# A four-layer attention and expert network on one core: the last attention in pairs of batches, and the last layer with its gate products first and one GpSimd step per piece

## The chip, the cores and the metric

The kernel runs on one core of one Trainium2 chip. A core has TensorE (PE: matrix products and turns), VectorE (DVE), ScalarE (ACT), GpSimd (POOL) and SyncE (SP, which here only issues DMAs). Each engine runs its own list of instructions in order and waits on semaphores. The time is the device time of one execution in microseconds; a lower one is better.

## The reference

Input are 16 batches of 128 tokens with 128 features, all float32, and a context `ctx_1024` of the same shape. There are four layers, each `x = x + attention(norm(x))` and then `x = x + feed-forward(norm(x))`. Three of the feed-forwards are mixtures of experts and hold most of the work. The change touches only the last attention and the last feed-forward:

```python
    x = x + _L3_xattn_ref(_layernorm(x, axis=-1), ctx_1024, ctx_1024, pos_1xS2)
    x = x + _L3_ffn_ref(_layernorm(x, axis=-1), L3_ffn_w_gate, L3_ffn_w_up, L3_ffn_w_down)
```

The attention has one head of 128. Two score matrices are made per batch, one with a positional table added to queries and keys (`pe[pos]`), one with other rows of that table (`pe[s_g_pos]`, `pe[g_pos]`); a fixed mask says per pair of positions which of the two counts, and the rest is causal:

```python
        attn = jnp.where(mask.astype(bool), ngb_attn, g_attn)
        w = jax.nn.softmax(attn, axis=-1)
        return jnp.einsum('bqk,bkd->bqd', w, v)
```

The feed-forward is a gated one, 128 to 384 and back, in which activations are rounded to 16 bits with a scale taken over the whole tensor:

```python
        def act_qdq(x):
            qmax = 2.0 ** (ACT_BITS - 1) - 1.0
            scale = jnp.maximum(jnp.max(jnp.abs(x)) / qmax, 1e-12)
            return jnp.clip(jnp.round(x / scale), -qmax - 1.0, qmax) * scale
        ...
        x = act_qdq(x)
        up = act_qdq(x @ lpbq_dequant(w_up).T)
        gate = act_qdq(x @ lpbq_dequant(w_gate).T)
        sig = fixed_qdq_u16(jax.nn.sigmoid(gate))
        gate = act_qdq(gate * sig)
        o = act_qdq(gate * up)
        return o @ lpbq_dequant(w_down).T
```

So five times a largest value over everything must be known before the next step can start: of x, up, gate, gate * sig, and o.

## The kernel before

Five engine programs are written out by hand, one per engine, and joined by semaphores. Stages have names: `l0x, l0f, l0m, l1x, l1f, l1m, l2x, l2m` are the attentions, inner attentions and expert layers of the first three layers; `l3x` is the last attention and `l3m` the last feed-forward. The tokens live in `X`, `[128 tokens, 16 batches, 128 features]`. There are eight PSUM banks of 512 columns: four `score_bank`, `turn_bank`, `out_bank` and two `f_bank`.

*End of l2m.* VectorE adds the experts' outputs to `X` in four chunks (`add`, L1927), takes the statistics of each batch (`measure`, L1597) and the variances (`variances`, L1606 and on); GpSimd takes the root (`power`, L702).

*l3x* runs batch by batch. The order of the steps on every engine is the table `ORDER["l3x"]`, in which Y is the normalising, F the queries and keys, S the scores, E the exponential, T the turn and V the weighing. Per batch: SyncE loads `cT` (L653) and `V128` (L657), 64 KB each. VectorE normalises the tokens into `y_tok` (L1689), TensorE turns them (L1188), VectorE adds the two positional tables (L1769, L1770), GpSimd adds two to the keys (L773, L774). TensorE puts the masks into a bank by a bf16 product (L1341) and adds two score products beside each other (L1343). VectorE copies one half (L1707), takes the maximum with the other (L1709: the mask has made the one that doesn't count very low), the largest value of a row (L1712), and subtracts it (L1716). ScalarE takes the exponential (L976), TensorE turns it (L1349), ScalarE copies it (L982), TensorE weighs the values (L1357) with a column of ones beside them, whose result is the sum. VectorE takes its reciprocal (L1723) and adds the scaled result to `X` (L1725), waits on it (L1732) and takes the new statistics.

*l3m* has these steps, each ended by a largest value (VectorE, L2029), an all-reduce over partitions (GpSimd, L911) and a few small steps on VectorE (`scale`):
- VectorE normalises 16 batches (L1633), one largest value over 2048 columns; TensorE turns the tokens (L1370), ScalarE rounds by adding a large number (`MAGIC`, 1.5 x 2^23; L1116), VectorE takes it off (L2037).
- 24 products of 512 columns (L1571) by two banks, three of up and three of gate for each of four chunks of tokens; ScalarE copies each out (L1122), VectorE takes the largest value of each. Both all-reduces follow together.
- Six pieces of 1024 columns (`HIDDEN_ORDER`): ScalarE rounds gate (L1127), up (L1127), and takes the sigmoid (L1134); VectorE takes MAGIC off gate (L2055), rounds the sigmoid (L2064), multiplies (L2066) and takes the largest value. GpSimd takes MAGIC off up (L920) and multiplies by up's scale (L921), two steps with two inputs each.
- ScalarE rounds again, VectorE multiplies with up (L2076), largest value.
- Rounding by VectorE and ScalarE in halves (L2087, L2088), the last product (L1579: 48 of 128x128, two records each), VectorE adds to `X` (L2092), SyncE stores (L669).

Where GpSimd goes from elementwise steps to an all-reduce or back, its instruction list has a row `ISA` without operands: the switch.

## Time and profile before

| | us |
|---|---|
| median of 3 runs (1544.35 to 1546.91) | 1546.83 |
| the profiled execution | 1546.87 |
| its span | 1545.1 |
| TensorE busy in the span | 1302.3 (84%) |
| VectorE | 987.3 (64%) |
| ScalarE | 726.6 (47%) |
| GpSimd | 499.0 (32%) |

The span goes from the first instruction to the last; the profiled execution's own time holds also what lies around it. The granted clock is the share of TensorE's full speed that the chip allowed; the mean here is 0.915, but the last stages stand apart. A row of a timeline is one instruction or a run of like ones: start, duration, engine, line, output and inputs, and in brackets how long its engine stood idle before it and what ended that. Matrix products of float32 leave more than one record each. In rows grouped by line the last field is the idle time before them.

### The profile page before, as it was taken

Reading aid. Unit: us, or ns where it says so; the run is one execution under the profiler, and the core shown is the slowest. Engines: PE = TensorE matmul, PEld = TensorE weight load, DVE = VectorE, ACT = ScalarE, POOL = GpSimd, SP = SyncE. Lnnn points to the kernel's source line nnn. Section 1 sums busy time; section 2 is a strip of 40 time slices with the busy share of each in tenths; the row PEclk is TensorE's granted clock in tenths of the full one; section 3 lists DMA queues with packets and bytes.
Section 4 is the critical chain, followed back from the end, with each engine's and each line's share of the span. In section 5 each row is a group of like instructions: output and inputs, shape, how many; then the busy total and the mean of one; then the engine's idle time right before and its main releaser. Section 6 shows DMA issues by size and latency. Waiting matters only on the chain.

```text
span 1545.1 us, 29908 instructions
## 1 busy us (share of the span) xinstructions
PE 1302.3 (84%) x9616; PEld 932.9 (60%) x9616; DVE 987.3 (64%) x2308; ACT 726.6 (47%) x2096; POOL 499.0 (32%) x544
## 2 busy tenths in 40 slices
PE   4888789999979999979988999889969799966603
PEld 3676677777755666557776777656645566644203
DVE  2766366676766555666775666656677845568696
ACT  3666156565634444447775777522212233321542
POOL 6500266666625000052213222120040057732070
PEclk9999699999999999999999999979988799965856
DMA  7000000000005555510000000012210066501000
GB/s 260 8 8 19 1 1 1 0 0 0 1 1 165 187 190 191 186 48 2 0 0 2 1 0 0 2 47 85 85 58 1 1 169 165 146 23 32 0 0 27
DMA packets 40086, 81.68 MB, mean 53 GB/s; under 512 B 5411, under 2 KB 22851, under 8 KB 39893
## 3 DMA queue, kind: packets, MB, share of 16 engines
q1 hardware_dynamic: 40020, 80.84, 16.7%
q8 instruction: 37, 0.61, 0.2%
q14 instruction: 29, 0.23, 0.1%
HBM read 79.18 MB, written 1.64 MB: 52 GB/s over the span
## 4 chain that ended last, share of the span: by engine, by line
PE 61%; DVE 14%; ACT 14%; issue 7%; POOL 2%; DMA 1%; ACTq 0%; DVEq 0%; SPq 0%; POOLq 0%
PE score_bank L1414 15%; ACT h_all L939 10%; PE f_bank L1443 7%; PE f_bank L1178 5%; PE score_bank L1259 5%; PE turn_bank L1275 4%; PE out_bank L1443 3%; PE turn_bank L1443 3%; PE out_bank L1315 3%; PE out_bank L1284 2%; PE score_bank L1250 2%; PE f_bank L1571 1%; PE out_bank L1324 1%; DVE work L1658 1%; PE f_bank L1199 1%
## 5 line engine op out<-in xcount | busy, mean ns | idle before, releaser
L1414 PE MATMUL score_bank<-parts 128*128 128x512 f32 x1040 | 396.2, 504 | 8.6 <-DVE parts L1792 7.1
L939 ACT ACTIVATE h_all<-score_bank,top_score 128x128 f32<-128x128 f32 x896 | 281.6, 401 | 114.7 <-DVE top_score L1646 114.6
L1414 PEld LDWEIGHTS score_bank<-parts 128*128 128x128 f32 x1040 | 202.2, 195 | 161.0 <-issue 115.0
L1646 DVE TENSOR_REDUCE top_score<-score_bank 128x4 f32<-128x512 f32 x224 | 142.9, 680 | 136.8 <-PE score_bank L1259 136.8
L1443 PE MATMUL f_bank<-h_all,wset 128*128 128x512 f32 x260 | 136.6, 607 | 14.7 <-DVE h_all L1889 12.9
L1877 DVE TENSOR_TENSOR h_all<-work,h_all 128x512 f32<-128x512 f32 x124 | 91.2, 738 | 85.8 <-ACT h_all L1043 85.7
L1043 ACT ACTIVATE h_all<-score_bank,wset 128x512 f32<-128x512 f32 x128 | 87.8, 687 | 116.1 <-PE score_bank L1414 116.0
L1275 PE MATMUL turn_bank<-CF,h_all 128*128 128x128 f32 x512 | 83.4, 286 | 42.7 <-DVE work L1658 23.2
L702 POOL TENSOR_TENSOR small<-small,half_neg 128x4 f32<-128x4 f32 (+2 forms) x22 | 36.3, 1655 | 241.3 <-DVE small L1619 128.6
L1275 PEld LDWEIGHTS turn_bank<-CF,h_all 128*128 128x128 f32 x512 | 56.3, 144 | 69.1 <-ACT h_all L939 22.7
L1039 ACT ACTIVATE rope_c<-score_bank 128x512 f32<-128x512 f32 x66 | 39.4, 597 | 112.6 <-PE score_bank L1414 99.4
L939 ACT ACTIVATION_READ_ACCUMULATOR h_all<-score_bank,top_score 128x1 f32 x384 | 91.9, 239 | 0.0
L1259 PEld LDWEIGHTS score_bank<-work 32*128 32x128 f32 (+1 forms) x2304 | 77.8, 187 | 22.9 <-issue 21.8
L1259 PE MATMUL score_bank<-work 32*128 32x128 f32 (+1 forms) x2304 | 90.0, 281 | 1.5 <-issue 1.2
L722 POOL TENSOR_TENSOR h_all<-h_all,prob_rec 128x512 f32<-128x512 f32 x64 | 66.3, 1046 | 75.1 <-DVE prob_rec L1650 75.1
L1039 ACT ACTIVATE shifted<-score_bank 128x512 f32<-128x512 f32 x66 | 39.3, 597 | 93.4 <-PE score_bank L1414 83.4
L1889 DVE TENSOR_TENSOR h_all<-score_bank,shifted 128x512 f32<-128x512 f32 x66 | 45.5, 691 | 43.8 <-POOL shifted L900 35.7
L1178 PE MATMUL f_bank<-yT,big 128*128 128x128 f32 x512 | 68.8, 285 | 1.4 <-ACT yT L996 1.4
L1579 PE MATMUL f_bank<-W3T,big 128*128 128x128 f32 x96 | 12.5, 298 | 67.6 <-DVE big L2088 67.6
L1443 PE MATMUL out_bank<-h_all,wset 128*128 128x512 f32 x130 | 66.3, 593 | 2.0 <-DVE h_all L1877 1.1
L1443 PE MATMUL turn_bank<-h_all,wset 128*128 128x512 f32 x130 | 67.2, 598 | 0.0
L1889 DVE TENSOR_TENSOR h_all<-score_bank,rope_c 128x512 f32<-128x512 f32 x66 | 45.4, 688 | 32.9 <-POOL rope_c L900 16.3
(360 smaller groups left out, 2748.4 us busy)
## 6 DMA issues: line engine op xcount, KB each, us to landing
work<-gates_l0m SPq DMA_DIRECT2D x62, 512.0 KB, 3.7
W0X<-gates_l2m SPq DMA_DIRECT2D x32, 256.0 KB, 3.8
CTX<-gates_l2m SPq DMA_DIRECT2D x32, 256.0 KB, 3.8
wset<-in_l0m SPq DMA_DIRECT2D x32, 128.5 KB, 3.4
W0X<-gates_l1m SPq DMA_DIRECT2D x8, 512.0 KB, 3.6
wset<-in_l1m SPq DMA_DIRECT2D x8, 384.0 KB, 3.1
CTX<-gates_l1m SPq DMA_DIRECT2D x6, 512.0 KB, 3.7
cT<-in_ctxT SPq DMA_DIRECT2D x32, 64.0 KB, 1.8
```

The source lines that it names most:

```text
L722: pool.tensor_tensor(probs4, probs4, wide(prob_rec[c][:, :], HEADS, P), ALU.mult).then_inc(normed, 1)
L939: last = act.activation(held[c][:, P * m:P * m + P], score_bank[c][:, P * m:P * m + P], ACT.Exp, bias=top_score[c][:, m:m + 1], **sums)
L1039: act.activation(act_sb[at][:, :], hid_bank[(c * H + h) % 2][:, :], ACT.Silu).then_inc(acted, 1)
L1043: act.activation(hT[at][:, :], hid_bank[at][:, :], ACT.Gelu, bias=wslot(M, s)[:, 2 * P:2 * P + 1]).then_inc(acted, 1)
L1178: last = pe_.matmul(bk[:, cols + P * q:cols + P * q + P], w[:, P * (m + q):P * (m + q) + P], x[:, :], start=True, stop=True)
L1259: last = pe_.matmul(banks[c][:, P * m:P * m + P], qT[slot][rows * c:rows * c + rows, at:at + P], kT[slot][rows * c:rows * c + rows, kat:ka ...
L1275: last = pe_.transpose(turn_dest(L, u)[:, P * m:P * m + P], held[unit_slot(L, u, s)][:, P * m:P * m + P], ident)
L1414: last = pe_.matmul(bk[:, :], wt[s % 2][:, col:col + P], y[:, x], start=(part == 0), stop=(part == len(parts_of) - 1))
L1443: pe_.matmul(sum_bank[c][:, :], wslot(M, s)[:, at:at + P] if n != "l2m" else wset[s][:, at:at + P], hT[(c * H + h) % 4][:, :], start=first ...
L1646: dve.tensor_reduce(top_score[c][:, :], split(score_bank[c][:, :], HEADS), AX_X, ALU.max, negate=True)\
L1877: dve.tensor_tensor(tile_at[:, :], by, tile_at[:, :], ALU.mult).then_inc(gated if M["gated"] else h_made, 1)
L1889: dve.tensor_tensor(hT[at % 4][:, :], hid_bank[2 + at % 2][:, :], act_sb[at % 4][:, :], ALU.mult).then_inc(h_made, 1)
```

## The change

*Loads.* The context comes once, whole: `ctxT` twice, into the two halves of `keys3` (a part of `work`), and `ctx` into `AO`, 3 MB in all, issued by SyncE behind the first weight loads of l2m. VectorE adds the positional tables to the keys inside l2m's first two sets of experts (`place_keys`, eight steps of 512 columns).

*End of l2m.* All four `add(c)` now stand behind the last expert step, and the normalising of l3x goes by quarters of four batches. GpSimd adds two small steps to each root (L701, L702 of the new file), so that ScalarE can normalise by scale and bias (`normalise`).

*l3x* runs by pairs of batches: 4 score products and one mask product fill one bank (`score3`), VectorE takes both batches' largest values in one step of 512 columns (`largest3`), ScalarE takes the exponential of both halves with the sum (`exponentials3`), and TensorE joins the two halves by turning both into one place (`turn_probs3`), after two products that only fill (`stream`). There is no copy, maximum or subtraction on VectorE any more, nothing on GpSimd and no load.

*l3m*: ScalarE normalises, the largest value goes by quarters; 8 and 12 filler products stand ahead of the 24, 16 ahead of the last product. The 24 go gate first, over eight banks. The order of the all-reduces is tokens, gate, up, gate * sig, o. The rounding of gate and the sigmoids start after gate's scale; ScalarE rounds pieces 0 and 1 of up with the last gate pieces, 2 to 5 behind the last sigmoid. GpSimd only takes MAGIC off, one step with one input per piece (L905); up's scale goes into the scale of the product. The last rounding goes by quarters, 3 x 512 columns each.

The diff, cut to what the prediction speaks of:

```diff
@@ GpSimd
+                    if name in ("l3x", "l3m"):
+                        link(last)
+                        link(pool.tensor_tensor(less_mean[:, lo:hi], mean[:, lo:hi], r1[:, lo:hi], ALU.mult))
+                        last = pool.tensor_scalar(shift[:, lo:hi], less_mean[:, lo:hi], -1.0, None, ALU.mult)
...
-            for n, count in enumerate([1, 2, 1, 1]):
+            for n, at in enumerate((0, 2, 1, 3, 4)):
                 pool.wait_ge(step("l3m.part_max"), n + 1)
...
-                if n == 1:
-                    pool.wait_ge(step("l3m.scale"), 3)
+                pool.partition_all_reduce(quant[:, at, 1:2], quant[:, at, 0:1], P, bass.bass_isa.ReduceOp.max)\
+                    .then_inc(step("l3m.all_max"), 1)
+                if n == 2:
                     for at, h in enumerate(HIDDEN_ORDER):
                         pool.wait_ge(step("l3m.u_round"), at + 1)
-                        u = U3[:, :, :].rearrange("p m t -> p (m t)")[:, 1024 * h:1024 * h + 1024]
-                        link(pool.tensor_tensor(u, u, magic.to_broadcast([P, 1024]), ALU.subtract))
-                        pool.tensor_tensor(u, u, quant[:, 1, 2:3].to_broadcast([P, 1024]), ALU.mult).then_inc(step("l3m.u"), 1)
+                        part = work[:, 1024 * h:1024 * h + 1024]
+                        pool.tensor_scalar(part, part, -MAGIC, None, ALU.add).then_inc(step("l3m.u"), 1)
@@ ScalarE
+            for c in range(4):
+                copies(1, c)
+            copies(0, 0)
+            act.wait_ge(step("l3m.scale"), 2)
+            for at in range(6):
+                rounded(big, at, 2, "l3m.g_round")
+                if at < 3:
+                    copies(0, at + 1)
+                if at == 4:
+                    act.wait_ge(step("l3m.scale"), 3)
+                if at >= 4:
+                    rounded(U, at - 4, 1, "l3m.u_round")
+                sigmoid(at)
+            for at in range(2, 6):
+                rounded(U, at, 1, "l3m.u_round")
@@ TensorE
+            def score3(j):
...
+                pe_.matmul(bk[:, :], ident_bf, own_bf.unsqueeze(1).to_broadcast([P, 2, 2 * P]), start=True, stop=False, skip_group_check=True)
+                for x in range(2):
+                    b = 2 * j + x
+                    for m in range(2):
...
+                        last = pe_.matmul(bk[:, cols], queries3[j // 2 % 2][:, b % 4, m, :], keys3[:, b, m, :],
+                                          start=False, stop=True, skip_group_check=True)
...
+            for j in range(2, PAIRS):
+                score3(j)
+                weigh3(j - 2)
+                turn_probs3(j - 1)
+                if j in (2, 4):
+                    fronts3(j // 2 + 1)
@@ VectorE
+                def place_keys(t):
+                    dve.wait_ge(in_keys, 16 * 3)
...
+                    dve.tensor_tensor(two, two, places, ALU.add).then_inc(placed3, 1)
...
+            for j in range(2, PAIRS):
+                largest3(j)
+                if j in (3, 5):
+                    queries3_of(j // 2 + 1)
+                add3(j - 2)
```

How the rows stand on an engine. GpSimd, from the last roots to the end, before (L911 the all-reduce, L920 and L921 the two steps per piece of up):

```order
L702 TENSOR_TENSOR small<-small,half_neg 128x12
L702 TENSOR_TENSOR small<-small,half_neg 128x4
L911 ISA
L911 ISA quant<-quant 128x1 x3
L920 ISA
L920 TENSOR_TENSOR work<-work,CF 128x1024
L921 TENSOR_TENSOR work<-work,quant 128x1024
```

The pairs of L920 and L921 repeat to the sixth, then come `L911 ISA` and two more all-reduces. After (L898 the all-reduce, L905 the one step per piece):

```order
L697 TENSOR_TENSOR small<-small,half_neg 128x12
L701 TENSOR_TENSOR small<-small 128x12
L702 TENSOR_SCALAR small<-small 128x12
L697 TENSOR_TENSOR small<-small,half_neg 128x4
L701 TENSOR_TENSOR small<-small 128x4
L702 TENSOR_SCALAR small<-small 128x4
L898 ISA
L898 ISA quant<-quant 128x1 x3
L905 ISA
L905 TENSOR_SCALAR work<-work 128x1024 x6
L898 ISA
L898 ISA quant<-quant 128x1 x2
```

The number of switches is the same, three. The two roots of l3m, of 12 and of 4 batches, have each got two small steps behind them; the second switch and the third stand around six steps in place of twelve.

TensorE inside the attention, before: two batches (L1341 masks, L1343 scores, L1349 turn, L1188 tokens, L1357 weighing):

```order
L1341 MATMUL score_bank<-CB 128x256
L1343 MATMUL score_bank<-work 128x128 x2
L1349 MATMUL score_bank<-CF,h_all 128x128
L1188 MATMUL f_bank<-CF,y_tok 128x128
L1357 MATMUL out_bank<-V_1,h_all 128x129
```

After: one pair (L1562 masks, L1567 scores, L1591 weighing, L1352 filler, L1582 turn):

```order
L1562 MATMUL score_bank<-CB 128x512
L1567 MATMUL score_bank<-work 128x128 x4
L1591 MATMUL score_bank<-AO,h_all 128x128 x2
L1352 MATMUL turn_bank<-CB 128x512 x2
L1582 MATMUL turn_bank<-CF,h_all 128x128 x4
```

One round now serves two batches: the scores of a pair stand ahead of the weighing of the pair two before it and the turn of the one before it.

ScalarE in the rounding stage, before (L1127 rounding: `big` is gate, `work` is up; L1134 sigmoid into `CTX`):

```order
L1127 ACTIVATE big<-big,CF,quant 128x1024
L1134 ACTIVATE CTX<-big,quant 128x1024
L1127 ACTIVATE work<-work,CF,quant 128x1024
L1127 ACTIVATE big<-big,CF,quant 128x1024
L1134 ACTIVATE CTX<-big,quant 128x1024
L1127 ACTIVATE work<-work,CF,quant 128x1024
L1127 ACTIVATE big<-big,CF,quant 128x1024
L1134 ACTIVATE CTX<-big,quant 128x1024
L1127 ACTIVATE work<-work,CF,quant 128x1024
L1134 ACTIVATE CTX<-big,quant 128x1024
L1127 ACTIVATE big<-big,CF,quant 128x1024 x9
```

After (L1138 rounding, L1144 sigmoid):

```order
L1138 ACTIVATE big<-big,CF,quant 128x1024
L1138 ACTIVATE work<-work,CF,quant 128x1024
L1144 ACTIVATE CTX<-big,quant 128x1024
L1138 ACTIVATE big<-big,CF,quant 128x1024
L1138 ACTIVATE work<-work,CF,quant 128x1024
L1144 ACTIVATE CTX<-big,quant 128x1024
L1138 ACTIVATE work<-work,CF,quant 128x1024 x4
L1138 ACTIVATE big<-big,CF,quant 128x1024 x6
```

The roundings of up were one behind each gate piece; now two stand among the last gate pieces and four behind the last sigmoid, and GpSimd's step needs each.

## Rows read from the trace of the kernel before

**Rows 1.** windows; us, busy (x count) of PE, PEld, DVE, ACT, POOL, clock, DMA:

```profile
40.00:60.00 20.00, 16.88 (x145) 13.07 (x144) 15.53 (x25) 12.71 (x47) 19.56 (x8) 0.98 0.03 9
1210.00:1220.00 10.00, 10.00 (x48) 9.63 (x47) 8.30 (x24) 3.84 (x6) 0.07 (x1) 0.50 0.00 0
1369.00:1428.00 59.00, 40.81 (x143) 27.79 (x143) 45.41 (x190) 9.38 (x32) 16.75 (x34) 0.50 0.12 35
1435.80:1464.40 28.60, 24.77 (x56) 9.33 (x56) 19.29 (x35) 17.33 (x28) 0.67 (x2) 0.92 0.00 1
1464.40:1508.10 43.70, 0.00 (x0) 0.00 (x0) 37.95 (x30) 21.75 (x19) 29.26 (x13) 0.50 0.00 0
1508.10:1525.40 17.30, 0.00 (x0) 0.00 (x0) 15.13 (x18) 6.90 (x6) 0.35 (x1) 0.50 0.00 0
1525.40:1545.10 19.70, 12.52 (x96) 12.33 (x96) 9.09 (x13) 3.50 (x3) 0.00 (x0) 0.82 0.18 53
```

**Rows 2.** chain of waits, the attention; start us, us, what:

```profile
1390.76 0.87 PE score_bank L1343 x4
1397.58 0.87 PE score_bank L1343 x4
```

**Rows 3.** lines by form, attention, TensorE; busy us, mean ns, idle before:

```profile
L1343 PE MATMUL score_bank<-work 128*128 128x128 f32 x64 | 17.0, 421 | 0.0
...
L1357 PE MATMUL turn_bank<-V,h_all 128*128 128x129 f32 x16 | 6.4, 500 | 0.7 <-ACT h_all L982 0.7
...
L1341 PE MATMUL score_bank<-CB 128*128 128x256 bf16 x16 | 6.2, 389 | 13.0 <-DVE work L1770 11.2 <-POOL work L774 1.8
```

**Rows 4.** timeline, end of the rounding stage; start us, us, engine, what:

```profile
1498.53 2.38 DVE L2064 TENSOR_SCALAR CTX<-CTX 128x1024 f32<-128x1024 f32 x1
...
1503.34 0.68 DVE L2064 TENSOR_SCALAR CTX<-CTX 128x1024 f32<-128x1024 f32 x1
1504.06 1.23 DVE L2066 SCALAR_TENSOR_TENSOR big<-CTX,big 128x1024 f32<-128x1024 f32 x1
1505.32 1.22 DVE L2029 TENSOR_REDUCE part_max<-big 128x1 f32<-128x1024 f32 x1
```

**Rows 5.** windows, inside the last product:

```profile
1533.00:1536.00 3.00, 3.00 (x30) 3.00 (x29) 0.69 (x1) 0.00 (x0) 0.00 (x0) 1.00 0.24 67
```

**Rows 6.** timeline, TensorE before the last experts:

```profile
1199.94 0.60 PE L1370 MATMUL f_bank<-CF,Y 128*128 128x128 f32 x4
...
1203.55 1.89 PE L1364 MATMUL turn_bank<-CB 128*128 128x512 bf16 x8
```

**Rows 7.** part 5 of the page, a 512-wide maximum:

```profile
L1646 DVE TENSOR_REDUCE top_score<-score_bank 128x4 f32<-128x512 f32 x224 | 142.9, 680 | 136.8 <-PE score_bank L1259 136.8
```

**Rows 8.** lines by form, attention, VectorE:

```profile
L1725 DVE SCALAR_TENSOR_TENSOR X<-turn_bank,recips,X 128x128 f32 x7 | 2.4, 350 | 1.0 <-DVE recips L1723 0.2
```

**Rows 9.** timeline, between the last experts and the attention:

```profile
1359.54 0.87 DVE L1597 BATCH_NORM_STATS2 st<-X 128x6 f32<-128x128 f32 x4
...
1367.93 1.09 POOL L702 TENSOR_TENSOR small<-small,half_neg 128x4 f32<-128x4 f32 x1 [0.24 <-DVE small L1621]
```

**Rows 10.** timeline, GpSimd around its all-reduces:

```profile
1435.04 0.38 POOL L911 PARTITION_ALL_REDUCE quant<-quant  x1 [5.84 <-DVE quant L2029]
...
1471.01 1.92 POOL L920 TENSOR_TENSOR work<-work,CF 128x1024 f32<-128x1024 f32 x1 [6.94 <-issue]
...
1506.87 0.38 POOL L911 PARTITION_ALL_REDUCE quant<-quant  x1 [6.51 <-DVE quant L2029]
```

**Rows 11.** lines by form, GpSimd, whole span:

```profile
L836 POOL TENSOR_SCALAR big<-big,GCOL 128x1024 f32<-128x1024 f32 x3 | 8.7, 2884 | 0.3
...
L860 POOL TENSOR_SCALAR MASK<-MASK 128x2048 bf16<-128x2048 bf16 x1 | 1.9, 1900 | 0.1
```

**Rows 12.** timeline, VectorE in the first experts of l2m:

```profile
1242.17 0.69 DVE L1889 TENSOR_TENSOR h_all<-score_bank,rope_c 128x512 f32<-128x512 f32 x1 [6.28 <-PE score_bank L1414]
```

**Rows 13.** DMA issues; times issued, KB each, us to landing:

```profile
W0X<-in_w0x SPq DMA_DIRECT2D x1, 1024.0 KB, 7.1
```

More of the change, by code:

```diff
@@ new lines, in _, with copies, piece, rounded @@
+            U = work
+            def copies(w, c):
+                for m in range(3):
+                    e = 12 * (1 - w) + 3 * c + m
+                    act.wait_ge(products_made, e + 1)
+                    act.activation((U3, G3)[w][:, m, BANK * c:BANK * c + BANK], ring8[e % 8][:, :], ACT.Copy)\
+                        .then_inc(products_copied, 1)
+            def piece(t, at):
+                h = HIDDEN_ORDER[at]
+                return t[:, 1024 * h:1024 * h + 1024]
+            def rounded(t, at, n, signal):
+                act.activation(piece(t, at), piece(t, at), ACT.Identity, scale=quant[:, n, 3:4], bias=magic).then_inc(step(signal), 1)
@@ new lines, in _ @@
+            add(0)
+            measured(0)
+            add(1)
+            measured(1)
+            queries3_of(0)
+            add(2)
+            largest3(0)
+            measured(2)
+            largest3(1)
+            add(3)
+            queries3_of(1)
+            measured(3)
+            for j in range(2, PAIRS):
+                largest3(j)
+                if j in (3, 5):
+                    queries3_of(j // 2 + 1)
+                add3(j - 2)
+            variances("l3m", 0)
+            add3(PAIRS - 2)
@@ new lines, in _, with largest, join_max @@
+            add3(PAIRS - 1)
+            variances("l3m", 1)
+            def largest(dst, src):
+                return dve.tensor_reduce(dst, src, AX_X, ALU.max, apply_absolute_value=True)
+            def join_max(last, n, cols):
+                link(last)
+                largest(quant[:, n, 0:1], part_max[:, cols]).then_inc(step("l3m.part_max"), 1)
+            for g in range(4):
+                dve.wait_ge(step("l3m.y"), g + 1)
+                last = largest(part_max[:, g:g + 1], Y[:, 4 * g:4 * g + 4, :].rearrange("p b d -> p (b d)"))
@@ L2014, in scale @@
+            join_max(last, 0, slice(0, 4))
             def scale(n, waits, unit=None):
@@ L2067, in _ @@
                 dve.wait_ge(step("l3m.gs"), at + 1)
-                last = largest(part_max[:, at:at + 1], part)
-            product_max(last, 3)
+                return largest(part_max[:, at:at + 1], piece(big, at))
+            for c in range(4):
+                last = chunk_max(1, c)
+            join_max(last, 2, slice(12, 24))
+            chunk_max(0, 0)
+            scale(2, 2)
+            gate_steps(0)
+            chunk_max(0, 1)
+            gate_steps(1)
+            chunk_max(0, 2)
@@ new lines, in _, with quarter, round_quarter, scale_quarter @@
+                dve.wait_ge(step("l3m.p"), at + 1)
+                last = largest(part_max[:, at:at + 1], piece(big, at))
+            join_max(last, 4, slice(0, 6))
+            scale(4, 5, 5)
+            dve.wait_ge(step("l3m.scale"), 5)
+            def quarter(q):
+                return G3[:, :, BANK * q:BANK * q + BANK]
+            def round_quarter(q):
+                link(dve.tensor_scalar(quarter(q), quarter(q), quant[:, 4, 3:4], MAGIC, ALU.mult, ALU.add))
+            def scale_quarter(q):
+                dve.tensor_scalar(quarter(q), quarter(q), MAGIC, quant[:, 4, 2:3], ALU.subtract, ALU.mult).then_inc(hidden_ready, 1)
```

472 lines of the change are left out of this document (234 added, 238 removed).

## The prediction

> **What bounds the kernel now.** The forecast is made against the profiled execution: 1546.87 us, of which 1545.1 us are the span, so 1.8 us lie around it. The median of the runs shown, 1546.83 us, is the same number. The change acts behind 1358.8 us, so I read that stretch, first the busy time by stage [rows 1]. The reader sees six stages: the last attention (59.0 us from 1369.0), the normalising of tokens (7.8, the gap before the next row), 24 products with their copies (28.6), rounding and sigmoid (43.7), the largest product (17.3), the last product and the store (19.7). [...]
>
> The chain of waits then shows the attention's beat: the score products of one pair of batches stand 6.8 us after those of the pair before (1390.76, 1397.58) [rows 2]. By form and line, one pair holds on TensorE 4 score products at 0.42, and per batch a mask product 0.39 and a weighing 0.50 [rows 3], a turn and a transpose of the same 128x128 size as a score product: 4 x 0.42 + 2 x (0.39 + 0.50 + 0.84) = 5.1 us of 6.8. The other 1.7 us are hand-overs between engines, since every batch passes them one by one.
>
> In the rounding stage the timeline shows VectorE and GpSimd slowing each other: the same 1024-wide step takes VectorE 2.38 us where GpSimd works and 0.68 where it rests [rows 4]. GpSimd is not the end of that stage: its all-reduce waits for VectorE.
>
> **The attention.** Removed per batch: VectorE's copy, maximum and subtraction, GpSimd's two key additions, two small loads. A pair now needs on TensorE one 512-wide bf16 mask product, 4 score products, 2 weighings, 2 bf16 filler products (512 wide) and 4 turns with the halves joined; twice in six pairs 4 transposes. At the upper clock a 128x128 f32 product is about 0.22 us (30 records in 3.00 us at clock 1.00 [rows 5], two records a product, so 0.20, and a little for the gaps between groups), the filler 0.236 (eight in 1.89) and four transposes 0.60 [rows 6]. So: mask 0.23 + scores 0.89 + weighings 0.45 + fillers 0.47 + turns 0.89 = 2.93, with hand-overs 3.2 us. At the lower clock the same list is 0.46 + 1.68 + 1.0 + 0.94 + 1.68 = 5.8, with hand-overs and transposes 6.5.
> VectorE has per pair a 512-wide maximum 0.68 [rows 7], two scaled additions of 0.35 [rows 8], two statistics of 0.22 (four in 0.87 [rows 9]) and a reciprocal: about 2.1 us, 3.3 where the queries of a quarter come too. ScalarE has two exponentials and a copy, 1.7. So TensorE stays the bound, with work lined up in front of it.
> Which clock? The rows speak both ways: TensorE 10.00 of 10.0 us busy at 0.50, 16.88 of 20.0 at 0.98 [rows 1], and in the stage of the last product, whose mean is 0.82 [rows 1], 1.00 is reached by 1533, 4 us behind its start [rows 5]. The attention before was broken by waits at 0.69 busy and stayed low; the new one is nearly continuous with the fillers. I take the upper level. Other end: 6.5 instead of 3.2 for the six pairs, +20 us.
> The start is not free. Additions and statistics of l2m's four chunks now stand together behind its last step: first addition at about 1359.2, 0.69 and 0.87 for addition and statistics and 1.0 for the variances, a root 1.09 [rows 9] and 0.5 for the two new small GpSimd steps, four normalisings on ScalarE 1.1, transposes 1.2 (cold), queries 1.2: queries at 1366.7, then three cold score groups held by the additions to 1375.9. Six pairs of 3.2 with two transposes of 0.6, and the last turn and weighing, end at 1398.2; the additions at 1399.6, variances 1400.55, root 1402.05.
>
> **The library switch.** Behind the root GpSimd's first all-reduce came 5.84 us after VectorE's last word for it, and the first subtraction 6.94 us after GpSimd had nothing to wait for; but the all-reduce at 1506.87 follows VectorE's maximum at once (0.3 us), as its switch ran while GpSimd stood idle [rows 10]. So a change between elementwise work and all-reduce costs some 6 us wherever nothing hides it. The first stays: 1402.05 + 5.85 = 1407.9, against a maximum ready at 1404.2; scale ready 1408.7 (1435.84 before): 27.1 us earlier.
> [...]
>
> **Products.** 24 products took 22.8 us (24.77 less the 1.97 of turns) at clock 0.92 [rows 1]: 0.86 each warm. The gate's twelve go first, so its scale waits for 12, not 24: start 1410, end 1421, copies, maximum, all-reduce and scale to 1426.5. That is 17.8 us instead of 28.6, and the other twelve run under the next stage.
>
> **Rounding and sigmoid.** Costs with GpSimd at rest: ScalarE 1.15 per 1024 columns (six in 6.90 [rows 1]) and a hand-over, VectorE 0.68 each for taking the rounding number off the gate and for rounding its sigmoid, 1.23 for their product, 1.22 for its largest value [rows 4]. Counted from the gate's scale: ScalarE has nine copies of the late products among its first rounds, and the maxima over them keep VectorE until 15.1. Its first piece (0.68 + 1.23 + 1.22, 3.2 with gaps), the other scale 0.8 and one gate step 0.7 end at 19.8, pieces 1 and 2 with their gate steps (3.9 each) at 27.6. GpSimd's first two subtractions lie from 27.5 to 34.2 and hold VectorE, so that piece 3 ends near 36.2 instead of 30.8, and the last gate step at 36.9. Sigmoid 5 ends at 38.1; the other four roundings of u stand behind it on ScalarE, so GpSimd starts its third subtraction at 39.4.
> What is a one-input GpSimd step of 128x1024 f32? The row is 2.88 us (the mean of three) [rows 11]; the immediate form on bf16, 2048 wide, took 1.90, 0.93 ns an element [rows 11], so the other end is 0.95 us. I take 2.83, hardly under the row of the same type and size. Four of them end at 50.7; then the switch, 6.3, is exposed, as the third all-reduce is now queued behind the last subtraction: 57.0, scale 58.1. So 58.1 us instead of 43.7, +14.4: the halved GpSimd work costs more than it saves, because half of it waits for ScalarE and a switch stands behind it.
> [...]
>
> **The rest.** Largest product: 17.3 as before. Round and scale: quarters of 1536 on VectorE, 2.1 us to the first instead of 3.7, up to 3.4 if the strided form is slower. Last product at the upper clock after 16 fillers 10.7 (48 x 0.22) instead of 12.52 [rows 1]; if the fillers don't bring the clock up, 12.5 again; last addition and store 3.4 as before. 16.2 instead of 19.7.
> The 8 key additions of 0.69 us lie among the experts of l2m, where VectorE idles (6.28 us ahead of its step at 1242.17 [rows 12]): nothing, 5.5 us if that cover were gone. The loads of 3.1 MB stand before l2m's gates, where the queues carried nothing (1210 to 1220: 0 GB/s [rows 1]).
>
> **Sum.** Before, from 1358.8: 77.0 + 28.6 + 43.7 + 17.3 + 19.7 = 186.3. After: 49.9 + 17.8 + 58.1 + 17.3 + 16.2 = 159.3. That is 27.0 less; I add 2 us for hand-overs not seen: 1546.9 - 25 = 1522. Nearly all of it is the attention.
>
> **Rivals.**
> 1. TensorE stays at the lower clock through the attention. For: [rows 1], 10.00 busy at 0.50. Against: 0.84 busy at 0.98, and the climb in [rows 5]. +20: 1542.
> 2. GpSimd's immediate form runs at 0.93 ns an element. [...] Then the u pieces keep ScalarE's pace (1.15), VectorE is not blocked, and the stage is 11 us shorter: 1511. Against: the 2.88 of [rows 11].
> 3. Slower. The key loads land late and VectorE waits at its first key addition inside l2m's first sets, with every expert step queued behind it. It decides if they land after some 1261, which is 50 GB/s for 3.1 MB from 1198. At the attention's 35 GB/s [rows 1] they land at 1287, l2m starts some 50 us late: about 1570. Against: 1 MB landed in 7.1 us at the start [rows 13].
> 4. The clock low and the l3m switch both exposed beyond the sum (a second switch in front of the tokens' all-reduce waits for VectorE): +20 and 3 to 6: inside 1544 to 1550, no change.
>
> **Chances.** Forecast 0.62, with its own range 1513 to 1531; rival 2 0.12; rival 1 0.15; rival 4 0.06; rival 3 0.03, and 0.02 for other mishaps on the slower side. A measurement tells about 0.2% (3 us) from no change, so no change is 1543.7 to 1550. Of rival 1 a fifth (0.03) lies there, of rival 4 two thirds (0.04), its rest is slower: faster 0.62 + 0.12 + 0.12 = 0.86, same 0.07, slower 0.02 + 0.03 + 0.02 = 0.07. The range 1509 to 1543 reaches from beyond rival 2 to the middle of rival 1 and leaves out rivals 3 and 4 and the edges, about 2 in 10.
>
> **What would show it.** Right: the granted clock at 0.9 or more from about 1378 to 1398, pairs 3.2 us apart; scale of the tokens near 1409 with GpSimd idle 5.8 us before its first all-reduce; six GpSimd steps of 2.8 us and then 6 us idle before the third all-reduce, so a rounding stage near 58 us; the last product in 10.7 us. Wrong: clock 0.50 in the attention; GpSimd steps near 1 us; VectorE idle for DMA at its key additions near 1240; or a stage of l2m that is longer than before.

## The result

The changed kernel took 1506.70 us, median of 4 runs (1504.82 to 1515.58), against 1546.87 us before (1544.35 to 1551.95). The ratio is 0.9748, 95% interval 0.9701 to 0.9794: faster. Forecast were 1522 us and a range of 1509 to 1543, so the time lies below the range. The profiled execution took 1504.82 us, span 1503.0, mean granted clock 0.945.

The windows of the changed kernel by stage; columns as in [rows 1]. The eight are: additions behind l2m; the attention's start; its six pairs; the tokens' scale; the gate's twelve products; rounding and sigmoid; the largest product; last product and store.

```profile
1348.20:1356.30 8.10, 3.03 (x18) 1.78 (x16) 6.04 (x27) 4.07 (x10) 2.94 (x6) 0.91 0.00 0
1356.30:1369.50 13.20, 11.05 (x54) 10.02 (x56) 8.73 (x33) 7.43 (x21) 2.94 (x6) 0.67 0.00 1
1369.50:1389.30 19.80, 18.39 (x140) 16.51 (x142) 13.17 (x45) 8.34 (x31) 2.38 (x2) 1.00 0.01 1
1389.30:1399.90 10.60, 7.09 (x26) 4.00 (x27) 5.08 (x18) 6.26 (x16) 2.23 (x6) 0.68 0.01 2
1399.90:1417.80 17.90, 17.90 (x48) 8.10 (x47) 11.12 (x13) 11.74 (x19) 0.35 (x1) 1.00 0.00 0
1417.80:1468.20 50.40, 5.03 (x12) 1.90 (x10) 30.24 (x36) 26.12 (x28) 17.96 (x8) 0.59 0.00 0
1468.20:1485.90 17.70, 4.66 (x15) 1.93 (x16) 15.20 (x19) 6.91 (x6) 0.35 (x1) 0.54 0.00 0
1485.90:1503.00 17.10, 11.34 (x98) 10.79 (x96) 10.08 (x10) 3.23 (x2) 0.00 (x0) 0.96 0.22 62
```

Read against [rows 1]: the stretch from the first addition (1348.2) to the tokens' scale (1399.9) is 51.7 us where it was 77.0. The products up to the first scale that lets the rounding start are 17.9 (28.6), the rounding stage 50.4 (43.7), the largest product 17.7 (17.3), the end 17.1 (19.7). Together 154.8 us in place of 186.3: 31.5 us less. The other 10.6 us of the 42.1 by which the two spans differ lie ahead of 1348.2.

TensorE in the attention, changed kernel, by the timeline; each L1562 row opens a pair. The rows begin with the third of the eight pairs, the first of the six of the third window:

```profile
1365.03 0.61 PE L1562 MATMUL score_bank<-CB 128*128 128x512 bf16 x1 [2.02 <-DVE work L2057]
...
1369.98 0.38 PE L1562 MATMUL score_bank<-CB 128*128 128x512 bf16 x1
1370.19 1.05 PE L1567 MATMUL score_bank<-work 128*128 128x128 f32 x8
...
1373.16 0.39 PE L1562 MATMUL score_bank<-CB 128*128 128x512 bf16 x1
...
1376.49 0.38 PE L1562 MATMUL score_bank<-CB 128*128 128x512 bf16 x1
...
1379.67 0.39 PE L1562 MATMUL score_bank<-CB 128*128 128x512 bf16 x1
```

The first pair shown still takes 4.95 us (8 records of scores in 1.92 us, from 1365.42: the lower clock, 0.50 in the column from 1365.03 to 1367.00). Behind it the same 8 records take 1.05 at the upper clock (1.00 from 1372 to 1386), and pairs come 3.18, 3.33 and 3.18 us apart, where [rows 2] had 6.8.

GpSimd in the changed kernel, timeline:

```profile
1399.16 0.38 POOL L898 PARTITION_ALL_REDUCE quant<-quant  x1 [6.02 <-issue]
1415.25 0.35 POOL L898 PARTITION_ALL_REDUCE quant<-quant  x1 [15.71 <-DVE quant L2101]
1431.26 0.72 POOL L898 PARTITION_ALL_REDUCE quant<-quant  x1 [15.66 <-DVE quant L2101]
1442.40 2.82 POOL L905 TENSOR_SCALAR work<-work 128x1024 f32<-128x1024 f32 x1 [10.42 <-ACT work L1138]
1446.09 3.08 POOL L905 TENSOR_SCALAR work<-work 128x1024 f32<-128x1024 f32 x1 [0.88 <-ACT work L1138]
1450.07 10.97 POOL L905 TENSOR_SCALAR work<-work 128x1024 f32<-128x1024 f32 x4 [0.91 <-ACT work L1138]
1466.97 0.38 POOL L898 PARTITION_ALL_REDUCE quant<-quant  x1 [5.92 <-issue]
```

What [rows 10] showed is there in its new places: 6.02 us of idle ahead of the tokens' all-reduce and 5.92 ahead of the fourth (the third behind the tokens'), and in neither does the profile name an engine that it waited for. VectorE's maximum had been ready 2.2 us before the one (1396.98) and 12.6 us before the other. The steps of one input take 2.82, 3.08 and 10.97 / 4 = 2.74 us, as [rows 11] had it; most of the last four lie behind VectorE's last step. VectorE beside them:

```profile
1442.48 1.53 DVE L2149 TENSOR_SCALAR CTX<-CTX 128x1024 f32<-128x1024 f32 x1
...
1446.43 1.24 DVE L2143 TENSOR_SCALAR big<-big 128x1024 f32<-128x1024 f32 x1
...
1448.31 1.23 DVE L2150 SCALAR_TENSOR_TENSOR big<-CTX,big 128x1024 f32<-128x1024 f32 x1
...
1451.69 1.23 DVE L2150 SCALAR_TENSOR_TENSOR big<-CTX,big 128x1024 f32<-128x1024 f32 x1
...
1454.20 0.16 DVE L2101 TENSOR_REDUCE quant<-part_max 128x1 f32<-128x6 f32 x1
```

A product step (L2150) takes 1.23 us beside a working GpSimd (1451.69), and the sigmoid's rounding 1.53 in place of 0.69. Of VectorE's steps beside GpSimd only the three simple ones (TENSOR_SCALAR) that began near a GpSimd step's start are longer, by 0.84, 0.56 and 0.26 us (1.53, 1.24 and 0.95, the last at 1450.71); products and largest values keep their 1.23 and 1.22. VectorE was at its end at 1454.4 and waited 13 us for GpSimd.

### The profile page after: what moved, and what is told of

It is laid out like the page before. It is cut to its first block, busy times and chain, and to the rows that moved or that the text cites. A ratio compares the mean times of both kernels' runs of the same rounds, so it can differ in the third digit from the quotient of the medians.

```text
span 1503.0 us, 29518 instructions
## 1 busy us (share of the span) xinstructions
PE 1284.3 (85%) x9665; PEld 930.1 (62%) x9708; DVE 951.5 (63%) x2176; ACT 740.5 (49%) x2135; POOL 477.8 (32%) x518
## 3 DMA queue, kind: packets, MB, share of 16 engines
q1 hardware_dynamic: 36996, 81.89, 17.3%
## 4 chain that ended last, share of the span: by engine, by line
PE 61%; ACT 15%; DVE 12%; issue 7%; POOL 3%; DMA 1%; ACTq 0%; DVEq 0%; SPq 0%; POOLq 0%
PE score_bank L1402 15%; ACT h_all L922 10%; PE f_bank L1431 7%; PE f_bank L1195 5%; PE score_bank L1273 5%; PE turn_bank L1289 4%; PE turn_bank L1431 3%; PE out_bank L1431 3%; PE out_bank L1329 3%; PE out_bank L1298 2%; PE score_bank L1264 2%; PE out_bank L1338 1%; DVE work L1730 1%; PE f_bank L1216 1%; DVE top_score L1718 1%
## 5 line engine op out<-in xcount | busy, mean ns | idle before, releaser
L1195 PEld LDWEIGHTS f_bank<-yT,big 128*128 128x128 f32 x512 | 63.2, 198 | 4.7 <-issue 3.1
L1431 PEld LDWEIGHTS f_bank<-h_all,wset 128*128 128x128 f32 x260 | 49.4, 192 | 26.6 <-DVE h_all L1918 12.3
```

The costliest lines, as they stand in the source:

```text
L1195: last = pe_.matmul(bk[:, cols + P * q:cols + P * q + P], w[:, P * (m + q):P * (m + q) + P], x[:, :], start=True, stop=True)
L1431: pe_.matmul(sum_bank[c][:, :], wslot(M, s)[:, at:at + P] if n != "l2m" else wset[s][:, at:at + P], hT[(c * H + h) % 4][:, :], start=first ...
```

## The experiments

Theory 1: the rounding stage came out shorter than forecast because a GpSimd step of one input hardly holds VectorE. Theory 2: most of the time gained ahead of the last experts is not the change's; it is when TensorE's clock rises in an execution. The rivals stand in the expectations. All ratios are to the kernel before.

**The changed kernel again**, unchanged.

> The changed kernel once more, unchanged. In its first profile the gates of l2m were ready at 1223.95 us, 9.7 us earlier than before the change (1233.66), in a part of the program whose work is the same. Theory A: those 9.7 us are when TensorE's clock was granted in that one execution; then this profile shows another time there, between 1224 and 1234, and the ratio to before comes out nearer to the 0.983 of the stages behind it than 0.975. Rival B: the change causes it; then the gates come at 1224 within 1.5 us, and the ratio is 0.974 again.

1509.24 us (1507.30 to 1511.61, 5 runs), ratio 0.9764, interval 0.9748 to 0.9780. The gates came at 1225.80, inside theory A's span and 1.85 us from the first profile. The ratio is not near theory A's 0.983, but that figure was too high: 0.983 is what the forecast's 27.0 us would give, while the stages behind the first addition measured 31.5 us less (186.3 to 154.8), which is 0.980, and 0.977 with the two repeated profiles (188.9 to 153.7). One run doesn't decide; the table below says more.

**The kernel before again**, unchanged.

> The kernel before once more. Theory A (the part ahead of l2m's experts varies with the execution): the gates of l2m, at 1233.66 in its first profile, come at another time, between 1224 and 1238. Rival B (the change moved that part): they come at 1233.7 within 1.5 us.

1545.89 us (1537.46 to 1550.25, 12 runs), ratio 0.9996 (0.9975 to 1.0017). From each profile three times are read: when the gates of l2m are ready, from there to the first addition behind l2m, and from there to the end of the span.

| profile | gates ready | to the first addition | to the end |
|---|---|---|---|
| before | 1233.66 | 125.2 | 186.3 |
| before again | 1233.60 | 125.1 | 188.9 |
| before, one GpSimd step | 1230.49 | 125.2 | 176.0 |
| before, fillers | 1227.27 | 124.7 | 189.7 |
| changed | 1223.95 | 124.2 | 154.8 |
| changed again | 1225.80 | 126.0 | 153.7 |
| changed, two inputs | 1229.44 | 125.8 | 152.3 |
| changed, no fillers | 1235.30 | 126.0 | 151.3 |
| changed, up on VectorE | 1229.50 | 125.1 | 142.4 |
| changed, up split | 1228.58 | 126.0 | 138.1 |

The times of the gates spread over 6 us in the four profiles of the old form and 11 us in the six of the new one, and the two overlap: 1227 to 1234 and 1224 to 1235. The two identical programs of before agree within 0.1 us, so this run by itself met rival B and not theory A. What speaks for theory A are the two other programs of the old form, whose instructions are the same up to the last attention and whose gates came at 1230.49 and 1227.27. The times of the runs say the same: the 12 runs of this one kernel go from 1537.46 us at a mean granted clock of 0.926 to 1550.25 at 0.911. The means of the gates, 1231.3 and 1228.8, differ by 2.5. One place where the spread arises is the stretch from 168 to 180 us, well ahead of the changed parts. Window of the kernel before (of it again the clock column is the same, 0.50):

```profile
168.00:180.00 12.00, 9.35 (x47) 7.13 (x46) 2.92 (x11) 1.05 (x3) 0.00 (x0) 0.50 0.00 0
```

The kernel before with fillers (an experiment below), whose instructions are the same up to there:

```profile
168.00:180.00 12.00, 7.63 (x50) 5.93 (x50) 3.84 (x16) 1.32 (x4) 2.12 (x6) 0.78 0.00 1
```

The changed kernel, and it without fillers in its attention (below):

```profile
168.00:180.00 12.00, 7.63 (x51) 5.93 (x50) 3.84 (x16) 1.14 (x3) 2.49 (x7) 0.78 0.01 2
```

```profile
168.00:180.00 12.00, 10.34 (x53) 8.42 (x53) 2.03 (x5) 1.05 (x3) 0.00 (x0) 0.50 0.00 0
```

So the column is 0.50 in three of these five profiles and 0.78 in two, and each value occurs with either form of the kernel. Of the other five the changed kernel again has 0.78 and four have 0.50; the three with 0.78 have the three earliest gates (1223.95 to 1227.27), the seven with 0.50 lie from 1228.58 to 1235.30, so this stretch makes a part of the spread and not all of it. So theory 2 holds for most of the 9.7 us: the forecast took over the early part from one execution, and the one that it was held against had it faster. What part is the change's stays open. GpSimd's first setup step behind the constants starts at 3.31 us in every profile of the old form and at 1.75 in every one of the new, but its first root starts at 12.7 to 14.6 and at 11.2 to 14.4, which overlap. By the runs the changed kernel is 36 to 39 us faster, by the stretch behind the first addition 31.5 to 35.2, so on average some us lie ahead of it, as the means of the gates also have it.

The column "to the first addition" answers rival 3: with the key additions among the experts it stays at 124.2 to 126.0 (124.7 to 125.2 without). The context's loads were issued from 1188.1 us on in the changed kernel and landed 8.5 and 11.6 us later, with 286 GB/s from 1190 to 1200, where rival 3 had reckoned with the old attention's 35.

**GpSimd's step with two inputs**, in the changed kernel:

```diff
-                        pool.tensor_scalar(part, part, -MAGIC, None, ALU.add).then_inc(step("l3m.u"), 1)
+                        pool.tensor_tensor(part, part, magic.to_broadcast([P, 1024]), ALU.subtract).then_inc(step("l3m.u"), 1)
```

> GpSimd takes the rounding number off with a step of two inputs (the number read from a table) in place of the step of one input. In the changed kernel VectorE's steps beside a one-input step took 1.53 and 1.24 us in place of 0.69, and pieces 2 to 5 of up started at +32.3 us behind the gate's scale. Theory A: it is the second input that holds VectorE; then VectorE's 1024-wide product and sigmoid steps beside GpSimd take 2 to 2.8 us again, the last sigmoid comes 2 to 4 us later, and GpSimd's own four steps at the end, alone, take 1.9 each in place of 2.74, so the stage from the gate's scale to the next (50.4) comes out at 48 to 51. Rival B: any GpSimd step holds VectorE alike and the changed kernel was only lucky in how they met; then VectorE's steps there stay at 1.2 to 1.5.

1508.25 us (4 runs), ratio 0.9742 (0.9721 to 0.9764). Timeline, VectorE and GpSimd:

```profile
1448.21 1.93 POOL L905 TENSOR_TENSOR work<-work,CF 128x1024 f32<-128x1024 f32 x1 [10.40 <-ACT work L1138]
1448.30 2.38 DVE L2149 TENSOR_SCALAR CTX<-CTX 128x1024 f32<-128x1024 f32 x1
...
1453.12 1.24 DVE L2143 TENSOR_SCALAR big<-big 128x1024 f32<-128x1024 f32 x1
...
1456.75 8.88 POOL L905 TENSOR_TENSOR work<-work,CF 128x1024 f32<-128x1024 f32 x4 [2.94 <-ACT work L1138]
...
1459.22 2.80 DVE L2150 SCALAR_TENSOR_TENSOR big<-CTX,big 128x1024 f32<-128x1024 f32 x1
...
1463.31 0.16 DVE L2101 TENSOR_REDUCE quant<-part_max 128x1 f32<-128x6 f32 x1
1471.43 0.38 POOL L898 PARTITION_ALL_REDUCE quant<-quant  x1 [5.81 <-issue]
```

VectorE's sigmoid rounding takes 2.38 us and its last product step 2.80, the very sizes that they had in the kernel before with GpSimd at work ([rows 4] shows the 2.38); with one input they were 1.53 and 1.23. So what theory 1 says of the step holds: one of two inputs holds VectorE for longer, 4.9 us in all against 1.7. But it doesn't explain the forecast's miss. Ahead of the last sigmoid only two steps of VectorE are lengthened in either run, and with two inputs the hold there is 1.69 + 0.56 = 2.3 us against 1.4: the last sigmoid comes 33.3 us behind the gate's all-reduce against 32.5, 0.9 us later and not the 2 to 4 that were expected. The rest of the longer hold lies behind it, where VectorE isn't the end of the stage. GpSimd's own four late steps take 8.88 / 4 = 2.22 us in place of 2.74 (expected were 1.9), so the stage is even shorter than with one input: from the gate's all-reduce to the fourth one 50.4 us against 51.7.

**One GpSimd step in the kernel before**, one part of the change alone: the two steps become one of one input, up's scale goes into the product's.

```diff
-                        link(pool.tensor_tensor(u, u, magic.to_broadcast([P, 1024]), ALU.subtract))
-                        pool.tensor_tensor(u, u, quant[:, 1, 2:3].to_broadcast([P, 1024]), ALU.mult).then_inc(step("l3m.u"), 1)
+                        pool.tensor_scalar(u, u, -MAGIC, None, ALU.add).then_inc(step("l3m.u"), 1)
```

> One part of the change alone: the kernel before, in which GpSimd has one step of one input per piece of up, and up's scale goes into the scale of the product. Theory A (a one-input step hardly holds VectorE): the rounding stage, 43.7 us, falls to 32 to 36, since VectorE's six pieces of 3.8 with some hold, plus 7 us at the start, set it, and all GpSimd steps end with them; the kernel 8 to 12 us faster. Rival B (a GpSimd step holds VectorE for as long as it lasts): pieces of 6.5 us, the stage at 40 to 42, and the kernel 2 to 4 us faster. Rival C: GpSimd's last step and the switch behind it become the end of the stage: 38 to 42.

1534.72 us (6 runs), ratio 0.9927 (0.9900 to 0.9954). Timeline:

```profile
1468.20 15.18 POOL L920 TENSOR_SCALAR work<-work 128x1024 f32<-128x1024 f32 x5 [6.97 <-issue]
1468.37 1.96 DVE L2065 SCALAR_TENSOR_TENSOR big<-CTX,big 128x1024 f32<-128x1024 f32 x1
...
1484.29 3.07 POOL L920 TENSOR_SCALAR work<-work 128x1024 f32<-128x1024 f32 x1 [0.91 <-ACT work L1126]
...
1492.13 0.16 DVE L2028 TENSOR_REDUCE quant<-part_max 128x1 f32<-128x6 f32 x1
1493.34 0.38 POOL L911 PARTITION_ALL_REDUCE quant<-quant  x1 [5.97 <-issue]
```

The all-reduce comes 32.8 us behind those before the stage (1460.56), where it was 43.5: 10.7 us less, theory A's 8 to 12. VectorE's pieces follow each other by 4.0 to 4.8 us in place of 7.4. The switch is nearly hidden: VectorE was ready 1.0 us ahead of the all-reduce. So in the old order one step of one input in place of two steps of two is worth 10.7 us; how much of that is the form and how much the count no run tells apart.

The same reading says what the new order does. From the tokens' all-reduce to the one that ends the rounding stage it is 71.8 us before, 61.0 here, and 67.8 in the changed kernel: its gate products first save 12 us of products, but from all-reduce to all-reduce the rounding stage is 18.9 us longer than here (51.7 against 32.8); 12.5 of them are the four late pieces and the switch behind them, as a run below shows. With the GpSimd steps where the change put them, the new order is dearer than the old one by 6.9 us.

**No fillers in the attention** of the changed kernel:

```diff
-                stream(2, bk)
                 pe_.wait_ge(exped3, j + 1)
```

> Without the two filler products ahead of each turn in the last attention (they compute nothing that is used). Theory A: the nearly continuous work alone is enough, and the granted clock rises at the same place or a little later; pairs come 2.8 us apart (3.2 less 0.47), and the attention is up to 3 us shorter. Rival B: the fillers bring the clock up; without them it stays at 0.50 through the attention, pairs come 5.0 us apart, and the attention is 10 to 14 us longer.

1508.12 us (4 runs), ratio 0.9749 (0.9732 to 0.9767). TensorE, timeline, the rows that open a pair:

```profile
1384.79 0.38 PE L1562 MATMUL score_bank<-CB 128*128 128x512 bf16 x1
...
1387.67 0.38 PE L1562 MATMUL score_bank<-CB 128*128 128x512 bf16 x1
...
1390.86 0.39 PE L1562 MATMUL score_bank<-CB 128*128 128x512 bf16 x1 [0.58 <-DVE work L2056]
```

The pairs of these rows are 2.88 and 3.19 us apart, at the upper clock (1.00 from 1381 to 1394; their scores take 1.05); over the last five intervals they go from 2.46 to 4.01, 3.1 in the mean, where theory A had 2.8. The same mean is 3.15 in the changed kernel's first profile and 3.3 in its second. From the first addition to the tokens' all-reduce it is 47.8 us, and 48.0 in the split version below, which has no fillers either, against 49.8 to 51.0 in the four profiles with them; the stretch to the end is 151.3 us against 154.8 and 153.7. The clock rises in the second pair's scores (8 records in 1.27 us where the first pair's took 1.91), as it does in the changed kernel's second profile (1.24 and 1.91). Theory A: the fillers are not what brings the clock up here, and the attention is some 2 us shorter without them.

**Fillers in the kernel before**, two products of 512 columns ahead of each batch's masks:

```diff
                         bk = s_bank[r]
+                        for _ in range(2):
+                            pe_.matmul(bk[:, :], ident_bf, causal_bf, start=True, stop=True)
```

> The kernel before with two filler products of 512 columns ahead of each batch's masks in the last attention, which compute nothing that is used. Theory A (continuous work brings the clock up): the granted clock rises above 0.9 and the attention falls from 59 to 48 to 53 us, VectorE's 45.4 us being the new bound. Rival B: it stays at 0.50, and the fillers, 0.94 us per batch, fill only the waits or make it up to 8 us longer.

1546.47 us (12 runs), ratio 1.0017 (0.9998 to 1.0035). The window of its attention:

```profile
1362.50:1421.50 59.00, 37.85 (x174) 23.74 (x175) 42.50 (x177) 9.39 (x32) 16.20 (x33) 0.82 0.12 34
```

TensorE's fillers in it (L1342), two batches apart:

```profile
1382.96 0.60 PE L1342 MATMUL score_bank<-CB 128*128 128x512 bf16 x2 [0.96 <-DVE work L1772]
...
1389.47 0.60 PE L1342 MATMUL score_bank<-CB 128*128 128x512 bf16 x2 [0.87 <-DVE work L1772]
```

Two of the waits (who waited for what, us in all, times, longest):

```profile
POOL work L773 <- DMA cT<-in_ctxT: 29.9, 11, 5.0
...
PE score_bank L1342 <- DVE work L1772: 13.9, 15, 1.6
```

The clock did rise, to a mean of 0.82 where it was 0.50, and the attention became no shorter: from the first addition to the tokens' all-reduce it takes 78.6 us, against 76.2 and 76.7 in the two profiles of before. Neither expectation. At the upper clock (1.00 from 1382 to 1390) a pair of batches takes 6.5 us (1382.96 to 1389.47) where [rows 2] had 6.8. TensorE still waits there for VectorE's work (0.96 and 0.87 us in these rows, 13.9 in all), and GpSimd waits 29.9 us for keys. But the fillers stand behind that wait and ahead of the masks, so they lie in the chain themselves: the masks follow 0.43 us behind the fillers' start, 0.9 us a pair. Less these, a pair at the upper clock would take some 5.6 us, an estimate from the two rows and the masks' start. So this run shows that fillers gain nothing in the old form; what a faster clock alone would be worth in it no run shows. It does show that most of the attention's gain is its form: with the upper clock and fillers in both, a pair takes 6.5 us in the old form and 3.2 in the new.

**Up's rounding number taken off by VectorE** in the changed kernel, GpSimd's loop removed:

```diff
+            def less_magic(at):
+                dve.wait_ge(step("l3m.u_round"), at + 1)
+                dve.tensor_scalar(piece(work, at), piece(work, at), MAGIC, None, ALU.subtract).then_inc(step("l3m.u"), 1)
...
             join_max(last, 3, slice(0, 6))
+            for at in range(6):
+                less_magic(at)
```

> VectorE takes the rounding number off the six pieces of up, behind its last gate piece; GpSimd has only its all-reduces in the last layer. Theory A: GpSimd's four steps of 2.74 us behind ScalarE and the switch of 5.92 us behind them are all that separates the last piece of gate (1454.3) from the all-reduce (1466.97); VectorE's six steps of 0.68 lie beside the all-reduce, so the stage is 50.4 less 12 to 14 us, and the kernel 12 to 14 us faster than the changed one (ratio to before about 0.966). Rival B: ScalarE's roundings (last at 1453.4) or VectorE's six steps come late; then the gain is under 8 us.

1498.83 us (5 runs), ratio 0.9693 (0.9673 to 0.9714). Timeline:

```profile
1458.06 0.16 DVE L2095 TENSOR_REDUCE quant<-part_max 128x1 f32<-128x6 f32 x1
1458.14 3.69 DVE L2162 TENSOR_SCALAR work<-work 128x1024 f32<-128x1024 f32 x6
1458.31 1.15 POOL L898 PARTITION_ALL_REDUCE quant<-quant  x1 [20.82 <-DVE quant L2095]
1461.75 0.20 DVE L2115 TENSOR_SCALAR quant<-quant 128x1 f32<-128x1 f32 x1
```

The all-reduce comes at once: 37.5 us behind the gate's, where it was 51.7. Of the 14.2 us, 12.5 are what GpSimd's four late steps and the switch behind them had cost, and 1.7 what its steps had held VectorE, whose last gate step now ends that much earlier. 2.6 of the 14.2 go to VectorE's six steps, behind which its scale waits until 1461.75. Net 11.6 us by the profile, some 10 by the runs; theory A was 12 to 14, a little too much for that reason.

**The same with the steps split**: VectorE takes pieces 0 to 2, ScalarE 3 to 5, and no fillers in the attention.

```diff
+            for at in range(3, 6):
+                act.wait_ge(step("l3m.u_round"), at + 1)
+                act.activation(piece(U, at), piece(U, at), ACT.Identity, bias=less_magic_col[:, :]).then_inc(step("l3m.u_act"), 1)
```

> A version meant to be the fastest: as the one in which VectorE takes the rounding number off up, but VectorE takes only pieces 0 to 2 and ScalarE, behind its last rounding, pieces 3 to 5 (1.15 us each), and the two filler products per turn of the attention are gone. In the run before, VectorE's scale came 3.4 us behind the all-reduce because six steps of 0.6 stood ahead of it. Theory A: three fewer give the scale 1.8 us earlier, ScalarE is free 3.5 us behind its last rounding of up, about when the scale comes, so 1 to 2 us less there, and 1 to 3 us less in the attention: last-layer and attention stretch (first addition to the end) from 142.4 to 138 to 140.5 us, kernel near 1495. Rival B: ScalarE becomes late for the rounding of the product and nothing is won in the last layer: 141 to 143.

1494.46 us (1493.73 to 1500.94, 5 runs), ratio 0.9687 (0.9660 to 0.9714). Timeline:

```profile
1454.89 3.21 ACT L1159 ACTIVATE work<-work,less_magic 128x1024 f32<-128x1024 f32 x3
...
1455.61 1.89 DVE L2166 TENSOR_SCALAR work<-work 128x1024 f32<-128x1024 f32 x3
1455.79 1.14 POOL L900 PARTITION_ALL_REDUCE quant<-quant  x1 [20.82 <-DVE quant L2099]
1457.41 0.21 DVE L2119 TENSOR_SCALAR quant<-quant 128x1 f32<-128x1 f32 x1
```

The scale comes 1.6 us behind the all-reduce in place of 3.4, ScalarE is free 0.2 us ahead of it, and the stretch to the end is 138.1 us: theory A. This is the fastest version here, 3.1% below the kernel before and 0.6 to 0.8% below the changed one by their ratios; against the version with VectorE alone the runs' intervals overlap, and only the profile shows the 4 us.

## Why the prediction was wrong

Predicted span 1520.1 (1522 less what lies around), found 1503.0: 17.1 us. By its own steps:

| step | predicted | found | difference |
|---|---|---|---|
| the part ahead of l2m's gates | as before | 9.7 less | -9.7 |
| gates to first addition (anchor 1359.2) | +0.4 | -0.9 | -1.3 |
| attention to the tokens' scale | 49.5 | 51.7 | +2.2 |
| products to the gate's scale | 17.8 | 17.9 | +0.1 |
| rounding and sigmoid | 58.1 | 50.4 | -7.7 |
| largest product | 17.3 | 17.7 | +0.4 |
| last product and store | 16.2 | 17.1 | +0.9 |
| hand-overs not seen | 2.0 | none | -2.0 |

*The step that failed* is an overlap in the rounding stage: "GpSimd's first two subtractions lie from 27.5 to 34.2 and hold VectorE, so that piece 3 ends near 36.2 instead of 30.8". It charged 5.4 us, nearly the whole length of the two steps (2 x 2.83). In the profile each of the two lengthens one step of VectorE, by 0.84 and 0.56 us, and the products and largest values beside them not at all: 1.4 us ahead of the last sigmoid. That is 4.0 us of the 7.7. It is not the number of inputs that makes it: with two-input steps in the same place the hold is 2.3 us, still less than half of 5.4, and the stage no longer. Another 3.0 or so lie in VectorE's chain apart from the hold, most of it because its first piece started at 13.3, not 15.1 us, and a piece with its gate step takes 3.7, not 3.9. The last 0.7 are mostly four steps of 2.74 in place of 2.83 and a switch of 5.9 in place of 6.3. What the forecast had right is what sets the end of the stage, four late pieces and an exposed switch: taking them away gave 12.5 us.

*The larger part of the miss* lies ahead of all that. The sum was made against one execution and took its first 1233 us as given, a term put at nothing without a reason, and 9.7 of the 17.1 us are there. Ten profiles show that part to vary by 11 us; which execution was the one shown before, and which the one after, was chance. The range (1509 to 1543) held only costs of the change and nothing for this; over the 9 runs of the changed kernel the median is 1508.7, at its lower edge. That the time came out near rival 2's 1511 is chance too: rival 2 needed GpSimd steps of 0.95 us, and they took 2.74 to 3.08.

*A reading of [rows 10] was wrong and did no harm.* The prediction has the first all-reduce 5.84 us "after VectorE's last word for it". The bracket is GpSimd's idle time; VectorE's maximum ended at 1434.50, 0.5 us ahead of the all-reduce:

```profile
1432.21 2.29 DVE L2029 TENSOR_REDUCE quant<-Y 128x1 f32<-128x2048 f32 x1
```

The 6 us of a switch count from GpSimd's last small step, and so the sum used them. The prediction calls it a library switch; what GpSimd does in that time no row shows. Shown are the row `ISA` in its list and 5.8 to 6.1 us of idle ahead of an all-reduce behind elementwise steps, where nothing hid them.

*What held.* The upper clock in the attention (1.00 from 1372 to 1389.3), with pairs 3.2 us apart. In this profile the third pair's scores were still at the lower one, which is 1.2 of the 2.2 us missed there; in the other five profiles of the new form that pair has the upper clock (1.05 us for its 8 records). The exposed first switch: from the last weighing to the scale 10.6 us, predicted 10.5. The gate's products to 0.1 us. The one-input step at 2.82 against the rival's 0.95: measured here, it is slower than the step of two inputs (means of six 2.83 and 2.14 us). The last product:

```profile
1496.73 2.84 PE L1651 MATMUL score_bank<-W3T,big 128*128 128x128 f32 x24
```

12 products (24 records) in 2.84 us at the upper clock (1.00 from 1496.70 to 1499.60), 11.0 in all, predicted 10.7 and with [rows 1] 12.52 before. No run takes away the 16 fillers ahead of it alone, so that they bring its clock up is not shown. The strided quarters of the rounding took 2.66 us to the first product, between the two ends given (2.1 and 3.4).

*Where the claim on the clock was right for a wrong reason*: the prediction gave the fillers a part in it. Without them the clock rises as well, in both versions that leave them out: it is 1.00 from 1381 to 1394 in the one and from 1371 to 1388 in the split one. Nor does any run show what makes it rise; that waits keep it down was the author's estimate from [rows 1], and with fillers in the old attention it rose to a mean of 0.82 with TensorE busy 37.85 of 59.0 us, where it was 0.50 with 40.81 busy.

## What to carry to other kernels

- Price a step on GpSimd by which of the neighbour's steps it meets, not by its whole length: the forecast charged VectorE 5.4 us for two GpSimd steps, and 1.4 (one input) or 2.3 (two inputs) were measured. And look at what stands behind its last step: a change back to an all-reduce cost 5.8 to 6.1 us where nothing hid it, so a few short steps on GpSimd can be dearer than the same steps on a busier engine (here six of them on GpSimd, 2.74 to 3.08 us each, cost 11.6 us more than on VectorE, which took 3.69 for all six).
- Fillers that stand in the chain can spend what a faster clock gives back: in the old attention the mean clock rose from 0.50 to 0.82 and the time did not fall (78.6 us from the first addition to the tokens' all-reduce, against 76.2 and 76.7). Ask first which engine's hand-over sets the beat.
- Take a change with several parts apart: here the cheaper GpSimd step was worth 10.7 us in the old order, and the new order gave 6.9 of it back.
- When a forecast rests on one execution, compare the untouched part of two or three executions first, and give the range that spread.

## What the runs showed that was not expected

- The step of one input with an immediate, 128x1024 f32, takes 2.74 us on GpSimd (mean of the four late ones, VectorE at rest for most of them) and up to 3.08 beside VectorE; the subtraction of two inputs takes 1.89 to 1.93 where it stands alone in the list, and 2.22 in the mean of the four late ones.
- Beside the one, VectorE's 1024-wide steps of 0.69 took 0.68 to 1.53 us and its product steps 1.22 to 1.96; beside the other up to 2.38 and 2.80. Its largest values took 1.22 beside either.
- The stretch from 168 to 180 us ran at a mean granted clock of 0.50 in seven executions and 0.78 in three, and the gates of l2m came at 1224 to 1235 us.
